# Match-replace on the raw correlation, the choice of weights by a comparison on VectorE, and a new loop order

## What is computed

```python
# 1: x -> 64 channels, four layers of (silu, scan over time, small MLP), back to 512 channels; residual, norm
# 2: cross attention by autocorrelation, for each channel over the 64 time steps:
corr = ifft(fft(q) * conj(fft(k))).real      # k, v: the context
w, idx = top_k(corr, 8)
w = softmax(w)
out = sum_i w[i] * v[min(idx[i] + pos, 63)]  # residual, norm
# 3: x quantized to 4 bits in blocks of 32 values (shared power-of-two scale,
#    values rounded to 0, 0.5, 1, 1.5, 2, 3, 4, 6 and their negatives), times a
#    weight quantized in the same way, plus a bias; residual, norm
```

## Time and profile before

| | us |
|---|---|
| median of 3 runs | 321.19 |
| lowest and highest run | 321.08, 324.42 |
| the profiled execution's own time | 323.65 |
| its span, first to last instruction | 321.6 |
| DVE busy | 269.8 (84%) |
| PE busy | 274.6 (85%) |
| ACT busy | 231.1 (72%) |
| POOL busy | 174.7 (54%) |
| mean granted TensorE clock | 0.978 |

### The profile page before, as it was taken

The page is one execution under the profiler, slowest core; times in us unless marked ns, Lnnn a source line. Parts: engine busy times, 40 slices in busy tenths (PEclk is TensorE's granted clock), DMA queues, the critical chain, the costliest instruction groups (busy, mean ns, idle before and its releaser), DMA issues.

```text
span 321.6 us, 4437 instructions
## 1 busy us (share of the span) xinstructions
PE 274.6 (85%) x1060; PEld 109.8 (34%) x1060; DVE 269.8 (84%) x871; ACT 231.1 (72%) x541; POOL 174.7 (54%) x226
## 2 busy tenths in 40 slices
PE   1597988989889887888998999999998888977762
PEld 1223222322222222254433554434444244422220
DVE  5969989889888894358999999999999989869580
ACT  6046789899799797967666687778877776745534
POOL 1026513204204014023378888999999999997842
PEclk9999899999999999999999999999999999979987
DMA  6999999602113200600000000111101102011122
GB/s 207 396 273 354 325 160 213 128 23 65 36 33 85 78 0 17 116 1 2 2 0 16 17 14 6 50 49 18 51 34 51 51 16 51 34 50 49 51 82 99
DMA packets 22576, 26.54 MB, mean 83 GB/s; under 512 B 10771, under 2 KB 11411, under 8 KB 22550
## 3 DMA queue, kind: packets, MB, share of 16 engines
q1 hardware_dynamic: 20470, 22.06, 21.9%
q0 software_dynamic: 2080, 4.19, 7.7%
HBM read 15.89 MB, written 4.19 MB: 62 GB/s over the span
## 4 chain that ended last, share of the span: by engine, by line
DVE 30%; ACT 20%; PE 18%; issue 15%; POOL 11%; DMA 3%; SPq 1%; POOLq 0%; DVEq 0%; ACTq 0%
DVE big L1172 5%; DVE m L1153 4%; DVE X L1107 3%; DVE big L1142 3%; DMA big<-in_xT_dram 3%; PE ps L380 3%; ACT big L654 3%; DVE ps L1203 3%; ACT L752 2%; DVE ps L1081 2%; ACT X L682 2%; PE ps L562 2%; POOL big L925 2%; POOL big L931 2%; DVE big L1277 2%
## 5 line engine op out<-in xcount | busy, mean ns | idle before, releaser
L654 ACT ACTIVATE big<-X,lnv 128x512 f32<-128x512 f32 x48 | 34.2, 713 | 15.0 <-DVE X L1107 15.0
L1107 DVE SCALAR_TENSOR_TENSOR X<-ps,X 128x512 f32<-128x512 f32 x48 | 32.1, 682 | 10.7 <-PE ps L415 6.1
L391 PE MATMUL ps<-ctx_ring,consts 64*128 64x512 f32 (+1 forms) x96 | 35.8, 643 | 0.0
L441 PEld LDWEIGHTS ps<-consts,big 96*128 96x128 f32 x256 | 29.8, 191 | 13.4 <-issue 10.6
L441 PE MATMUL ps<-consts,big 96*128 96x64 f32 x256 | 32.0, 278 | 1.1 <-DVE big L1142 1.1
L1184 DVE TENSOR_TENSOR big<-ps,ctxf 128x512 f32<-128x512 f32 x48 | 30.8, 683 | 2.0 <-PE ps L475 1.3
L682 ACT ACTIVATE X<-X,lnv 128x512 f32<-128x512 f32 x32 | 25.8, 808 | 0.6
L1172 DVE MATCH_REPLACE8 big<-w,big 128x64 f32<-128x64 f32 x128 | 25.1, 210 | 0.0
L838 POOL TENSOR_TENSOR big<-big 128x512 f32<-128x512 f32 x4 | 5.8, 1444 | 35.5 <-DVE big L1250 25.5
L918 POOL TENSOR_TENSOR big<-big 128x512 f32<-128x512 f32 x15 | 19.0, 1268 | 6.2 <-DVE big L1172 6.0
L1142 DVE TENSOR_TENSOR big<-ps,ctxf 96x512 f32<-96x512 f32 x32 | 20.4, 677 | 0.8 <-PE ps L428 0.8
(11 more groups left out here) (188 smaller groups left out, 675.9 us busy)
## 6 DMA issues: line engine op xcount, KB each, us to landing
big<-in_xT_dram SPq DMA_DIRECT2D x4, 1024.0 KB, 9.4
ctx_ring<-in_ctx_dram SPq DMA_DIRECT2D x16, 256.0 KB, 4.0
out_dram<-X SPq DMA_DIRECT2D x16, 256.0 KB, 2.0
X<-in_x_dram SPq DMA_DIRECT2D x2, 1536.0 KB, 11.4
X<-rows_sb POOLq DMA_DIRECT2D x1, 3072.0 KB, 21.6
X<-in_wq_dram SPq DMA_DIRECT2D x1, 1024.0 KB, 5.6
X<-in_x_dram SPq DMA_DIRECT2D x2, 512.0 KB, 3.9
X<-rows_sb POOLq DMA_DIRECT2D x1, 1024.0 KB, 8.0
```

Of the source, the lines that this page charges most:

```text
L391: mm(bank(LANE_BANK[lane]), mat((CY_0, CY_1, CY_C)[f])[half, :], ctx_ring[half, r * N:(r + 1) * N], start=True, stop=True).then_inc(s_cfor ...
L441: last = mm(ps[:, 2 * N + j * P + b * L:2 * N + j * P + (b + 1) * L], PQ[0:EVEN, b * N + j * P:b * N + (j + 1) * P], mat(IC_E)[0:EVEN, 0:L ...
L654: squared[k, n] = chain(a(JUNK[k], row(n), ACT.Square, bias=st[:, 0:1], scale=-float(V), accum_out=st[:, 2:3]))
L1107: stt(row(m), bank(b), 0.0, row(m), ALU.add, ALU.add, accum_out=st[:, 0:1]).then_inc(s_sum[k], 1)
```

## The change

The eight maxima are now taken out of `CR`, the raw correlation, instead of out of `G`: `largest_taken` runs the same eight match-replaces on `CR` with the maxima in `m8` and writes -3e38 (`TAKEN`) into their places in `REST`. `w8`, its subtraction on POOL and its exponential on ACT go. `chosen` moves from POOL to DVE: one SCALAR_TENSOR_TENSOR, `(REST == TAKEN) * G`, for all pairs. Of `rounding`, the exponent field stays on DVE as `exponents`, now a TENSOR_TENSOR of `VB` and a one-column constant `field`, from SBUF to SBUF; the `max` and multiply go to POOL as a third instruction in front of the clamp. All loops have a new order and new offsets, some stages run one or two iterations earlier, the copy `CR` is freed by the match-replace, and the last block of the weight transposes moves from bank 4 to bank 7. The filler matmuls are 10 and 12, each behind the feed-forward of its iteration.

```diff
-DRAIN_BUSY = ((0, 4), (6, 6), (5, 3))
+DRAIN_BUSY = {LAST + 6: 10, LAST + 7: 12}
...
@@ SP @@
-            for n in range(PAIRS + 3):
+            for n in range(PAIRS + 5):
                 quantized_to_channels(n)
-                stored(n - 3)
+                stored(n - 5)
...
@@ PE, feed_forward @@
-                    pe.wait_ge(s_magic[1], min(n + 2, LAST))
+                    if n == 0:
+                        pe.wait_ge(s_hn, 2)
...
@@ PE, the loop @@
-            for t in range(1, PAIRS + 11):
-                weights_to_time(t - 7)
-                out_even(t - 8)
-                weight_rest_forms(t - 7)
-                weight_forms(t - 7)
-                correlation(t - 5)
-                if t == 5:
-                    transposes(0, VC, bank(4), XQ[0])
-                query_forms(t - 4)
-                feed_forward(t - 10)
-                if t == LAST + 7:
-                    pe.wait_ge(s_sum[0], PAIRS)
-                if LAST + 7 <= t < LAST + 10:
-                    kept_busy(DRAIN_BUSY[t - LAST - 7][0])
-                if t == 5:
-                    pe.wait_ge(s_qe[0], VC)
+            for t in range(1, PAIRS + 9):
+                out_rest(t - 6)
+                weights_to_time(t - 5)
+                out_even(t - 6)
+                weight_rest_forms(t - 5)
+                weight_forms(t - 5)
+                projection(t)
+                if t == 1:
+                    mixed(SLOTS)
+                    transposes(0, VC, bank(7), XQ[0])
+                if t == 4:
                     pe.wait_ge(s_sq1, SLOTS + 2)
                     mm(bank(4), mat(MEAN), SQ_LAST, start=True, stop=True).then_inc(s_var1, 1)
-                quantized_to_channels(t - 9)
-                if LAST + 7 <= t < LAST + 10:
-                    kept_busy(DRAIN_BUSY[t - LAST - 7][1])
-                out_rest(t - 7)
-                projection(t)
-                if t == 2:
-                    mixed(SLOTS)
+                correlation(t - 3)
+                quantized_to_channels(t - 8)
+                feed_forward(t - 8)
+                query_forms(t - 2)
+                if t in DRAIN_BUSY:
+                    pe.wait_ge(s_sum[0], PAIRS)
+                    kept_busy(DRAIN_BUSY[t])
...
@@ ACT @@
-                        act.wait_ge(s_m8, n - 1)
+                        act.wait_ge(s_mr, n - 1)
...
-                    a(w8[:, :], w8[:, :], ACT.Exp).then_inc(s_g, 1)
                     a(G, G, ACT.Exp).then_inc(s_g, 1)
...
-            for t in range(PAIRS + 10):
-                squares(0, t)
-                corr_out(t - 3)
-                if t == 3:
-                    weight_channels(VC - 1)
-                squares(2, t - 9)
-                if t == 2:
+            for t in range(PAIRS + 8):
+                if t == 1:
                     act.wait_ge(s_mlp, SLOTS)
                     a(SQ_LAST, XC[1], ACT.Square, bias=base[:, DEPTH:DEPTH + 1]).then_inc(s_sq1, 1)
+                squares(0, t)
+                probabilities(t - 3)
+                corr_out(t - 2)
+                last_factors(t - 8)
+                factors(0, t)
+                weights_out(t - 3)
+                top_exponentials(t - 2)
+                normalise(0, t)
+                if t == 1:
+                    weight_channels(VC - 1)
+                log_sum(t - 2)
                 quantized_out(t - 7)
-                factors(0, t - 1)
-                top_exponentials(t - 3)
-                weights_out(t - 4)
-                log_sum(t - 3)
-                normalise(0, t - 1)
-                last_factors(t - 9)
-                squares(1, t - 5)
-                factors(1, t - 5)
-                normalise(1, t - 5)
-                if t == 4:
+                squares(2, t - 7)
+                squares(1, t - 4)
+                factors(1, t - 4)
+                if t == 3:
                     act.wait_ge(s_var1, SLOTS + 2)
...
-                probabilities(t - 3)
+                normalise(1, t - 4)
...
@@ POOL @@
-                    chain(g_.tensor_tensor(groups(w8[:, :], TOP), top, sh.broadcast_to([P, NG, TOP]), ALU.subtract))
...
-            def chosen(n):
-                    g_.tensor_tensor(WN, G, REST, ALU.subtract).then_inc(s_wn, 1)
...
             def clamped(n):
+                    pool.wait_ge(s_expo, n + 1)
+                    chain(g_.tensor_scalar(MB, MB, 0.25, MAGIC, ALU.max, ALU.mult))
+                    chain.then_wait(g_.tensor_scalar(VB, VB, 1.5, -1.5, ALU.min, ALU.max))
+                    halfway[n] = chain(g_.tensor_tensor(VB, VB, MB, ALU.add))
...
-            for t in range(PAIRS + 8):
-                block_scaled(t - 3)
-                chosen(t - 1)
+            for t in range(PAIRS + 9):
+                block_scaled(t - 4)
+                finished(t - 9)
+                differences(t - 1)
+                clamped(t - 4)
+                rounded_off(t - 4)
                 top_differences(t)
-                finished(t - 7)
-                mark = clamped(t - 3)
-                differences(t)
-                rounded_off(t - 3, mark)
...
@@ DVE @@
+            ch(v_.memset(field[:, :], EXPONENT))
...
-            def without_largest(n):
-                    dve.wait_ge(s_g, 2 * n + 2)
+            def largest_taken(n):
+                    dve.wait_ge(s_m8, n + 1)
                     for g in range(NG):
-                        last = v_.match_replace(REST[:, g * L:(g + 1) * L], w8[:, g * TOP:(g + 1) * TOP],
-                                                G[:, g * L:(g + 1) * L], 0.0)
+                        last = v_.match_replace(REST[:, g * L:(g + 1) * L], top[:, g * TOP:(g + 1) * TOP],
+                                                CR[n % 2][:, g * L:(g + 1) * L], TAKEN)
...
-            def rounding(n):
+            def exponents(n):
-                    do(ts(bank(1).bitcast(I32), VB.bitcast(I32), 0x7F800000, None, ALU.bitwise_and))
-                    ts(MB, bank(1), 0.25, MAGIC, ALU.max, ALU.mult).then_inc(s_magic[1], 1)
+                    tt(MB.bitcast(I32), VB.bitcast(I32), field[:, 0:1].broadcast_to([P, V]), ALU.bitwise_and
+                       ).then_inc(s_expo, 1)
...
+            def chosen(n):
+                    dve.wait_ge(s_g, n + 1)
+                    dve.wait_ge(s_mr, n + 1)
+                    stt(WN, REST, TAKEN, G, ALU.is_equal, ALU.mult).then_inc(s_wn, 1)
...
             for t in range(PAIRS + 9):
+                top_sum(t - 4)
+                crossed(t - 6)
+                exponents(t - 7)
+                last_quantized(t - 7)
+                largest_taken(t - 4)
+                weight_products(t - 5)
+                block_scales(t - 6)
                 attended(t)
-                weight_products(t - 6)
-                block_scales(t - 7)
-                without_largest(t - 5)
-                last_chosen(t - 5)
-                fed(t - 9)
-                last_quantized(t - 7)
-                largest(t - 4)
-                if t == 6:
+                if t == 5:
                     last_norm(1, RS_LAST)
-                rounding(t - 7)
-                top_sum(t - 4)
-                query_products(t - 3)
-                crossed(t - 6)
+                chosen(t - 4)
+                largest(t - 3)
+                fed(t - 8)
+                query_products(t - 2)
```

More of the change, by code:

```diff
@@ L38 @@
 HEAD = 32
+TAKEN = -3.0e38
+EXPONENT = 0x7F800000
 SPLIT = 3
@@ L192, in build @@
         e8 = sb("e8", [P, NG * TOP])
-        w8 = sb("w8", [P, NG * TOP])
         den = sb("den", [P, 3 * NG])
@@ L197, in build @@
         ends = sb("ends", [P, NBLK], I32)
+        field = sb("field", [P, 1], I32)
         xq = sb("xq", [P, V], BF16)
@@ L463, in weight_rest_forms @@
                     if n == 0:
-                        pe.wait_ge(s_act, 4 * SLOTS)
+                        pe.wait_ge(s_qe[0], VC)
                     if n >= 1:
@@ L907, in differences, with rounded_off @@
                     chain.then_wait(g_.tensor_tensor(sh, top[:, :, 0:1], den[:, NG:2 * NG].unsqueeze(2), ALU.add))
-                    chain(g_.tensor_tensor(groups(w8[:, :], TOP), top, sh.broadcast_to([P, NG, TOP]), ALU.subtract))
                     g_.tensor_tensor(groups(G, L), groups(CR[n % 2], L), sh.broadcast_to([P, NG, L]),
                                      ALU.subtract).then_inc(s_gs, 1)
-            def chosen(n):
-                if here(n) and n < LAST:
-                    pool.wait_ge(s_mr, n + 1)
-                    if n >= 1:
-                        pool.wait_ge(s_wt, n)
-                    g_.tensor_tensor(WN, G, REST, ALU.subtract).then_inc(s_wn, 1)
+            halfway = [0] * PAIRS
             def clamped(n):
                 if here(n) and n < LAST:
-                    pool.wait_ge(s_magic[1], n + 1)
+                    pool.wait_ge(s_expo, n + 1)
+                    chain(g_.tensor_scalar(MB, MB, 0.25, MAGIC, ALU.max, ALU.mult))
                     chain.then_wait(g_.tensor_scalar(VB, VB, 1.5, -1.5, ALU.min, ALU.max))
```

(6 more changed lines are left out.)

18 lines of the change are left out of this document (7 added, 11 removed).

## The result

The changed kernel takes 333.28 us (median, 333.06 to 335.22), the kernel before beside it 321.24 (321.08 to 324.42): a ratio of 1.036, with a 95% interval of 1.030 to 1.042. The forecast was 316.6 with a range to 323.5, so it was wrong in sign and by more than the range.

The account below looks back on a forecast made before the run. A ring through VectorE and ScalarE's layernorm set the 9.94 us period; VectorE's sum came next. -0.8 - 2.7 - 1.1 - 1.2 + 1.2 = -4.6 against 321.6 gave 317.0, or 316.6 from the median; range 311 to 323.5.

Parts of the forecast that it names:

- GpSimd's sum: GpSimd's work per period: 9.15 less 1.27 and 0.30, plus one 0.61, is 8.2; 8.7 us with gaps, 9.7 with stretches.
- The shared side: VectorE's `exponents` and `chosen`, two SBUF inputs each, meet GpSimd: VectorE waits little, GpSimd loses up to 0.5 us twice.
- the near end of its bounds: Period with contention lies between 9.64 and 10.9 us; 9.78 taken, by the layout and TensorE's 9.7.
- rival 3: Port decides: both VectorE instructions miss their gap, 10.9 us for seven periods, 10.3 for three; 328.8 us; chance 0.15.
- Who wins a meeting: At the shared SBUF side, the second to come waits, and VectorE wins even when it starts 0.1 us late.
- The ring: VectorE's block scales wait on `crossed` and ScalarE's layernorm, 3.30 + 6.64 = 9.94 us; the new order makes that wait nothing.
- VectorE's sum: VectorE's work per period: 9.94 less 0.21 of waiting and 1.31 of `rounding`, plus 1.22 for two instructions, 9.64 us.
- TensorE: TensorE's period, same computation with new neighbours among the matmuls: between 9.52 and 9.78 us, taken as 9.7.
- The fill: Start of the pipeline: first search 0.8 us earlier, and pair 0 to pair 5 in 40.4 instead of 43.15, 2.7 gained.
- Pairs 5 to 15: Seven periods with all stages gain 1.1 us; three without `attended`, 9.55 against 9.94, gain 1.2.
- The drain: After pair 15's search: quantization delays of 1 to 2 us, fillers 2.75, about 2 won; taken as 1.2 longer.
- The chances: Forecast 0.45, rivals 0.15, 0.25 and 0.15; faster by over 1% 0.55, within 1% 0.30, slower 0.15.

Follow-up runs that it names:

- e4: The changed kernel with one memset and eight 128x512 tensor_scalar instructions of differing operations put into GpSimd's idle start; ran once, 335.68 us.
- e5: The changed kernel with the maximum and multiply moved from GpSimd back to VectorE behind the exponents, SBUF to SBUF; 331.85 us, ratio 1.027.
- e6: The changed kernel with GpSimd's max-and-multiply split into two passes, (min, max) and (multiply, add); 330.82 us, ratio 1.026.
- e8: The changed kernel with both edits, GpSimd's two fast passes (e6) and the match-replace output in PSUM (e7); 321.7 us, ratio 1.000.
- e10: The changed kernel with the old rounding put back whole on VectorE, exponents into bank 1, maximum and multiply out of it; 325.48 us, ratio 1.011.
- e1: The changed kernel with GpSimd's max-and-multiply swapped to multiply, then max with the scaled constant; 337.64 us, ratio 1.045.
- e7: The changed kernel with REST, the match-replace output, in PSUM bank 3 instead of SBUF; 329.18 us, ratio 1.021.
- e11: e10 with REST, the match-replace output, in PSUM as in e7; 325.92 us, ratio 1.012.
- e9: The changed kernel without the twelve filler matmuls in front of the last transposes; 331.99 us, ratio 1.029.
- e12: e8 without the twelve filler matmuls in front of the last transposes; 320.29 us, ratio 0.995.
- e13: e12 with the maximum and multiply of pairs 12, 13 and 14 on VectorE instead of GpSimd; 320.06 us, ratio 0.994.
- e2: The changed kernel with GpSimd's max-and-multiply done as integer max and add on the bit patterns; 336.66 us, ratio 1.044.

## Why the prediction was wrong, step by step

- **GpSimd's sum: the step that failed.** "One more 0.61 like L924 comes" took a row of the same form (one input, one output, 128x512, two operations with constants) for a price that depends on the two operations. It is 1.92, fifteen times, so 19.7 us more work on an engine that the forecast put at 8.7 of 9.78, and at 9.7 with its stretches. The text gave this cost no upper bound. The trace of before had no row of a max and multiply on GpSimd, but it had a warning outside the loop. L868 is a multiply alone, by a column, and takes 0.92 to 1.43 for half as many elements as L924 does in 0.61 (min, median and max ns of four; VectorE works beside them, so the shortest counts most):

```profile
L868 POOL TENSOR_SCALAR w1d<-w1d,raw x4: 919/1141/1434, 26.9 to 30.6; 128x256 f32<-128x256 f32 x4
```

e4's multiply alone on 128x512, 1.49, is in line with it. With 1.92 the forecast's own sum gives 8.7 + 1.31 + 1.0 = 11.0 for the period, and 10.75 was measured.
- **The shared side: right in kind, wrong in its layout.** The two losses of 0.3 and 0.5 from the earlier trace rows came back as 0.33 (L922) and 0.52 (L932), and in VectorE's place as 0.81 (`chosen`). `exponents` won by starting 0.03 behind L932, as laid out. `chosen` was to fall into the gap in front of the dequantization and fell into L916, two instructions ahead of it. GpSimd was 2.7 us late by then. L914 makes up 1.31; the rest was there before it, since `differences` ends 3.5 us behind the head of VectorE's iteration (227.61 against 224.09) where 2.2 was laid out. The forecast took the near end of its bounds, 9.78, and said that a lag of 0.3 would change it. e5 and e6 show that without the slow pair the layout would have failed as well (10.82, 10.79). The mechanism is that of rival 3, though rival 3 left out the pair's own price.
- **Who wins a meeting: one row made into a rule.** "VectorE wins even when it starts 0.1 late" was drawn from one row, behind L941, and was then used for the dequantization. It holds behind that step, `finished` (e8: VectorE 0.12 and 0.13 behind it, 0.68 and 0.69 long). Behind the others it doesn't: 0.13 behind the dequantization `chosen` took 1.46 (e10, shown above), and 0.09 behind L916 it took 1.73 (e1). The Trainium skill, "SBUF — State Buffer", section "Who interferes with whom", says that the shared ports are an exclusive lock, and that the order of issue and not the shape of the operation decides who blocks. The traces agree for L916 and the dequantization, where the second to come lost at every lag. They don't for VectorE starting 0.03 to 0.13 behind `finished` (L941 before, L932 after) and winning, unless that one's recorded start lies ahead of its first read, which no run here settles.
- **The ring: right.** In the steady part no block scale waits for the normalise any more. In e8, where GpSimd is no longer in the way, the early periods are 9.54, and in e7 too (9.54 and 9.55), so VectorE's and TensorE's floors allow this. The gain was there.
- **VectorE's sum: right.** 9.64 was forecast. e11's 10.27 less its two roundings (226.83 - 225.50 = 1.33) plus one `exponents` of 0.61 is 9.55.
- **TensorE: too dear.** 9.7 was taken, and e8's periods of 9.54 show that TensorE needs no more than that, beside the 9.52 of the earlier trace rows. The new neighbours cost nothing that shows.
- **The fill: right.** 40.70 from pair 0 to pair 5 (139.93 to 180.63) where 40.4 was forecast and 43.15 was before. The first search at 139.0 can't be judged, since that moment moves between 138.1 and 140.7 from run to run.
- **Pairs 5 to 15: the sign turned.** 103.7 us where the forecast had 97.1 and before 99.5: three periods of 9.93, four of 10.75, one of 9.40 and two of 10.74.
- **The drain: mis-sized by 8.5 us.** GpSimd's chain per pair is 9.0 to 9.3 there, not 7. Two parts were measured. The slow pair costs 3.8 (e6 against the changed kernel) and the fillers 1.4 (e9), of which the forecast had named the second ("lost in full") at 2.75. The rest of the 9.7 is about 4.5. With the maximum and multiply off GpSimd altogether (e10) the drain is 5.8 shorter and not 3.8, so some 2.0 of the rest still come from where they stand. (e5, which has them on VectorE from SBUF to SBUF, gains only 3.3.) About 2.5 are then left for the new order, which no run tested by itself. From the search of pair 15 to the start of GpSimd's clamping (or maximum) of pair 12 it is 2.5 us before, 4.8 in e10, 6.9 in e8 and 7.8 in the changed kernel. The forecast counted three roundings "still before them, as before", but the first of them was nearly due in the old order and isn't in the new. In e12, without the slow pair and the fillers, the drain is 5.0 us longer than before: 4.4 until that point, 1.1 less for the rounds of pairs 12 and 13 (16.9 against 18.0), 1.6 more from the round of pair 14 to the end (20.3 against 18.7). The last pair's quantization lasted 5.1 us before (307.48 to 312.57) and 8.4 now (312.76 to 321.15); 3.3 of delay is over the 1 to 2 that were expected and over the 3 that the forecast gave as its limit. Its one-input instructions from SBUF to SBUF were stretched too: the one that took 0.43 before took 1.15 beside GpSimd.
- **The chances.** 0.15 stood on slower, and all of it on the shared side. No chance was given to GpSimd's sum being wrong, though its new instruction had no row of its own. (The +6.9 in rival 3 is 6.7 by its own 10.9 per period, which changes none of this.)

## What to carry to other kernels

An operation that the trace doesn't show on that engine has no known price, even where a row of the same shape and form stands beside it: give it an upper bound, and ask what the engine's sum would be by it. Look for rows of the same operation on that engine in other parts of the program, too. When an engine runs without a pause, every meeting on a shared resource finds it under way, so shortening one engine may only hand the wait to the other; test the two remedies together before either is judged. Moving one operand of the VectorE instruction to PSUM took the meeting away almost for nothing here. A step moved later in the order should be followed through the drain, pair by pair, from the last common event.

e13 and e12 are the fastest of all, by about half a per cent: 0.994 (0.991 to 0.997) and 0.995 (0.992 to 0.998) of the kernel before.

## What the runs showed of the hardware

- GpSimd's tensor_scalar on 128x512 f32 takes 0.61 to 0.66 for the pairs min and max, add and multiply, multiply and add, and 1.49 to 1.95 for a max or a multiply alone and for max followed by a multiply or add (e4); multiply followed by max took 2.20 in e4 and 1.92 in e1. Integer max and add takes 1.92 too (e2). Doing more in one instruction can be quicker than doing less: multiply alone 1.49, multiply and add 0.66 (e4), and 0.62 with an add of 0.0 (e6). The Trainium skill, "GPSIMD Engine Reference", section "3.1 Elementwise — side-by-side cycle accounting", states 1.03 cycles per element for the shortest loop bodies and, as the best case of a tight loop, about 1.8, which is 0.77 us for 512 elements. The rows at 0.61 to 0.66 are quicker than that best case, L941's 0.77 is equal to it, and those at 1.5 to 2.2 agree with neither figure. The section doesn't tell the operations apart.
- When VectorE takes two inputs from SBUF beside a GpSimd instruction, one of the two is held until the other is done, and it can be either. In e5 VectorE ended 0.53 and 0.55 after GpSimd's end; in the changed kernel GpSimd's L932 came out 0.52 longer. The second to come loses where GpSimd's instruction is a TENSOR_TENSOR of 128x512. Behind the one that finishes a row (L932) VectorE won at lags of 0.03 to 0.13, and behind one of 128x8 at 0.21 (e8: GpSimd's 0.20 became 0.96). In e5, at a lag of 0.78 behind the same instruction, both came out longer (1.27 for 0.77, 1.02 for 0.69).
- VectorE's one-input instructions from SBUF to SBUF are held up by GpSimd too: 0.43 alone, 1.15 beside it (e5, and the last pair of the changed kernel).
- Match-replace into PSUM is almost as fast as into SBUF: 0.212 to 0.218 (e7, e8, e11) against 0.203 to 0.210.
